# The first half's work up to FFN layer h1 ahead of the branch on exact weights, and FFN weights loaded in place

## The reference

```python
x = x + attn(xn) + ffn(xn)

def attn(h):                     # gated linear attention, keys 64, inner width 512
    x, final_gate = h @ up_w.T, h @ gate_w.T
    shift = silu(causal_conv4(x, conv_w) + conv_b)
    q, k = shift @ q_w.T, shift @ k_w.T
    v = sigmoid(x @ ig_w1.T @ ig_w2.T + ig_b2) * x
    g, tau = softplus(shift @ g_w.T + g_b), sigmoid(shift @ tau_w.T + tau_b)
    kn = k / norm(k) * g ** tau
    o = chunk_scan(q * 64 ** -0.5, kn, v, -g * tau) + shift * residual_weight
    xg = o * silu(final_gate)
    return (xg * rsqrt(mean(xg ** 2) + eps) * norm_weight) @ down_w.T

def ffn(h):                      # weights are -1, 0 or 1; s are scales per output
    h = silu(h @ w1.T * s1) * (h @ w2.T * s2)      # 256 -> 1024
    h = gelu(h @ h1.T * sh1)                       # 1024 -> 1024
    h = gelu(h @ h2.T * sh2)                       # 1024 -> 1024
    return h @ w3.T * s3                           # 1024 -> 256
```

## Time and profile before

| | |
|---|---|
| median of three runs | 1940.59 us |
| lowest, highest | 1940.5, 1941.85 us |
| profiled execution: its time, its span | 1940.21, 1938.4 us |
| TensorE busy | 1921.8 us (99%), 16804 matmuls |
| VectorE busy | 1584.1 us (82%) |
| ScalarE busy | 1295.3 us (67%) |
| granted TensorE clock, mean | 0.998 |

### The profile page before, as it was taken

How to read it: one execution, slowest core, us unless ns; L and a number is a source line. 1 busy time by engine, 2 the same in 40 slices (tenths; PEclk the granted TensorE clock), 3 DMA queues, 4 the chain that set the end, 5 groups by cost and what they waited for, 6 DMA issues and landing times.

```text
span 1938.4 us, 46120 instructions
## 1 busy us (share of the span) xinstructions
PE 1921.8 (99%) x16804; PEld 1902.9 (98%) x16804; DVE 1584.1 (82%) x4304; ACT 1295.3 (67%) x2687; POOL 81.2 (4%) x136
## 2 busy tenths in 40 slices
PE   8999999999999999999999999999999999999998
PEld 7999999999999999999999999999999999999998
DVE  7788888888788887888888788787888878888887
ACT  5666667767676766666766667675667666667575
POOL 0000000000000000000000000000000000000000
PEclk9999999999999999999999999999999999999999
DMA  8000000000000000000000000000000000000000
GB/s 309 7 12 13 12 2 12 12 12 12 13 1 12 13 12 12 8 5 13 12 13 12 7 6 12 13 12 13 1 12 13 12 12 12 1 13 12 13 7 8
DMA packets 23538, 34.19 MB, mean 18 GB/s; under 512 B 3170, under 2 KB 19810, under 8 KB 23364
## 3 DMA queue, kind: packets, MB, share of 16 engines
q1 hardware_dynamic: 23364, 31.43, 4.8%
HBM read 23.04 MB, written 8.39 MB: 16 GB/s over the span
## 4 chain that ended last, share of the span: by engine, by line
PE 94%; issue 2%; ACT 1%; DVE 1%; SPq 1%; DMA 0%; POOLq 0%; POOL 0%; DVEq 0%; ACTq 0%
PE fb L383 64%; PE ab L383 21%; PE ab L593 2%; PE ab L628 1%; PE ab L529 1%; PE ab L453 1%; PE ab L518 1%; PE ab L583 1%; PE fb L678 1%; SPq L289 0%; PE ab L590 0%; PE ab L469 0%; PE ab L606 0%; ACT wwhole L726 0%; DMA sgate<-stage_w 0%
## 5 line engine op out<-in xcount | busy, mean ns | idle before, releaser
L383 PE MATMUL fb<-hid1h,wwhole 128*128 128x256 f32 x2048 | 474.2, 279 | 0.1
L383 PE MATMUL fb<-hid1l,wwhole 128*128 128x256 f32 x2048 | 467.9, 276 | 0.0
L383 PE MATMUL fb<-hid0l,wwhole 128*128 128x256 f32 x2048 | 465.9, 276 | 0.0
L383 PE MATMUL fb<-hid0h,wwhole 128*128 128x256 f32 x2048 | 465.8, 276 | 0.0
L383 PEld LDWEIGHTS fb<-hid1h,wwhole 128*128 128x128 f32 x2048 | 384.5, 188 | 4.0 <-ACT raw L838 0.3
L383 PEld LDWEIGHTS fb<-hid1l,wwhole 128*128 128x128 f32 x2048 | 384.7, 188 | 0.0
L383 PEld LDWEIGHTS fb<-hid0h,wwhole 128*128 128x128 f32 x2048 | 384.5, 188 | 0.0
L383 PEld LDWEIGHTS fb<-hid0l,wwhole 128*128 128x128 f32 x2048 | 384.4, 188 | 0.0
L838 ACT ACTIVATE raw<-fb,sh_s 128x256 f32<-128x256 f32 x512 | 212.3, 465 | 150.3 <-PE fb L383 142.7
L383 PE MATMUL fb<-xntl,wwhole 128*128 128x256 f32 x1024 | 237.5, 276 | 0.0
L383 PE MATMUL fb<-xnth,wwhole 128*128 128x256 f32 x1024 | 237.5, 276 | 0.0
(11 more groups left out here) (234 smaller groups left out, 4481.6 us busy)
## 6 DMA issues: line engine op xcount, KB each, us to landing
xin<-x SPq DMA_DIRECT2D x32, 256.0 KB, 2.7
out<-xin SPq DMA_DIRECT2D x32, 256.0 KB, 2.2
stage_more<-stage_w SPq DMA_DIRECT2D x6, 512.0 KB, 7.1
sgate<-stage_w SPq DMA_DIRECT2D x4, 512.0 KB, 4.4
shift<-stage_w SPq DMA_DIRECT2D x4, 512.0 KB, 5.0
v<-stage_w SPq DMA_DIRECT2D x4, 512.0 KB, 5.6
raw<-stage_w SPq DMA_DIRECT2D x3, 512.0 KB, 6.0
mixed<-stage_w SPq DMA_DIRECT2D x3, 512.0 KB, 8.2
```

Source lines behind the costliest of these rows:

```text
L383: mm = pe.matmul(o, a, b, start=start and i == 0, stop=stop and i == len(pairs) - 1)
```

## The change

SP issues all chunks without a wait, each to a place of its own: the FFN chunks to where their rounded form will be (`wplain` is the plain f32 view of `wwhole`), the others to `stage` (over `hid1h`, `hid1l`) and `small`. Comb and gate move to the front of the order. Constants are split: 14 early ones two behind each of the first seven chunks, seven late ones one behind each later chunk.

A half is cut in two functions on each engine. `before` runs from z to proj, `after` from h1 to the end. For the first half `before` stands ahead of the branch, with some differences (`first`): layer1 multiplies the plain f32 weights by the plain f32 `xplain` (one plain matmul in place of two rounded ones), gate stands ahead of layer1, and ScalarE and VectorE have tests and roundings between its steps. The loops run `after`, `before` for each half. The unread matmuls are gone.

The test of an FFN chunk no longer compares with the rounded copy. It looks at the low 16 bits of each weight, read as uint16 with a step of two: ScalarE copies them to a scratch tile with their sum as accumulated output (`flag`, 18 chunks), or VectorE takes their maximum by a reduce (four chunks, `DVE_FLAGS`). A chunk whose low bits are all zero is exact. After its test a chunk is rounded in place by VectorE (`round_whole`). `ACT_FLAGS`, `ACT_LAST`, `DVE_ROUNDS` and `DVE_LAST` say which chunk is tested or rounded at which place. The late part, `ACT_LAST` and `DVE_LAST`, stands between `before` of the first half and the branch.

```diff
-CHUNKS = (["up"] + [f"w1{k}" for k in range(2)] + [f"w2{k}" for k in range(2)] + ["gate", "proj", "comb"]
+CHUNKS = (["up", "comb", "gate"] + [f"{w}{k}" for w in ("w1", "w2") for k in range(2)] + ["proj"]
           + [f"h1{k}" for k in range(8)] + ["down"] + [f"h2{k}" for k in range(8)] + ["w30", "w31"])
+ROUNDED = ("up", "comb", "gate", "proj", "down")
...
+ACT_FLAGS = {"first": ("w10", "w11", "w20", "w21"), 0: ("h10",), 1: ("h11",), 2: ("h12",), 3: ("h13",), 4: ("h14",), 5: ("h15",), 6: ("h16",)}
+ACT_LAST = ("h17", "down", "h20", "h22", "h23", "h25", "h26", "w30")
+DVE_ROUNDS = {1: ("h10",), 2: ("h11",), 3: ("h12",), 4: ("h13",), 5: ("h14",), 6: ("h15",), 7: ("h16",)}
+DVE_FLAGS = ("h21", "h24", "h27", "w31")
+DVE_LAST = ("tables", "w10", "w11", "w20", "w21", "h17", "down", "h21", "h20", "h22", "h24", "h23", "h27", "h25", "h26", "w31", "w30")
+ACT_FLAGGED = [name for names in (*ACT_FLAGS.values(), ACT_LAST) for name in names if name != "down"]
...
+        wplain = at_same_place("wplain", [P, len(WHOLE), STAGE], F32, wwhole_place)
...
-        stage_more = at_same_place("stage_more", [P, 2, STAGE], F32, hid1_place)
-        ig2raw = at_same_place("ig2raw", [ZK, DI], F32, hid1_place + 4 * FB * N)
+        stage = at_same_place("stage", [P, 4, STAGE], F32, hid1_place)
 
         mixed = sb("mixed", [P, 4 * N])
+        ig2raw = mixed[0:ZK, 0:DI]
...
+        xplain = work[:, DB * N:DB * N + HB * N].rearrange("p (h t) -> p h t", h=HB)
...
+        EARLY = ([(ident_s, ident), (ig1w, ig1t), (convw_s, convw), (convb_s, convb), (ig2raw[ZB:ZB + 1, :], ig2t[R:R + 1, :]),
+                  (ig2raw[ZB + 1:ZK, :], ig2t[R:R + 1, :])] + [(ig2raw[i * R:(i + 1) * R, :], ig2t[0:R, :]) for i in range(6)]
+                 + [(s1_s, s1), (s2_s, s2)])
+        LATE = [(projb_s, projb), (normw_s, normw), (resw_s, resw), (sh1_s, sh1), (sh2_s, sh2), (s3_s, s3),
+                (pair_mask, masks[:, LEVELS - 1, :])]
+
+        def stage_of(name):
+
+            if name == "comb":
+                return small[:, 0:STAGE]
+            return stage[:, ("up", "gate", "proj", "down").index(name), :] if name in SPLIT else wplain[:, WHOLE[name], :]
+
+        def low_bits(name):
+
+            return stage_of(name).bitcast(mybir.dt.uint16).rearrange("p (o two) -> p o two", two=2)[:, :, 0]
+
...
-            for n in range(len(CHUNKS)):
-                if n == SLOTS - 1:
-
+            early, late = iter(EARLY), iter(LATE)
+
+            def constants(some, count, landed):
+                for dst, src in itertools.islice(some, count):
+                    sp.dma_start(dst[:], src).then_inc(landed, 16)
+
+            for n, name in enumerate(CHUNKS):
+                sp.dma_start(stage_of(name), stage_w[n]).then_inc(stage_in[name], 16)
+                if name == "up":
                     sp.dma_start(xin[:, 0, :, :], x[0]).then_inc(x_in[0], 16)
-                    for dst, src in CONSTS:
-                        sp.dma_start(dst[:], src).then_inc(const_in, 16)
-                if n >= SLOTS:
-
-                    sp.wait_ge(prep_act, n - SLOTS + 1)
-                    sp.wait_ge(prep_dve, n - SLOTS + 1)
-                sp.dma_start(stage_slot(n), stage_w[n]).then_inc(stage_in[n % SLOTS], 16)
+                constants(early, 2, const_in)
+                if n >= len(EARLY) // 2:
+                    constants(late, 1, late_in)
...
-
-            def plain(bank, count, weights_at=0, moving_at=0):
-                for i in range(count):
-                    w, t = weights_at + (i // 2 % 6) * P, moving_at + (i % 2) * N
-                    pe.matmul(fb[bank][:, 0:N], up[:, w:w + P], w10[:, t:t + N], start=(i == 0), stop=(i == count - 1))
...
-                                   ig1w[:, d, :], start=(d == 0), stop=(d == DB - 1))
-            mm.then_inc(prep_pe, 1)
 
             def ln_transpose(me, first=False):
                 pe.wait_ge(xn_d.sem, xn_d.at(me))
@@ -453,16 +453,24 @@
                         mm = pe.transpose(ab[2][:, h * N + c * CH:h * N + (c + 1) * CH], xn[:, c, h * P:(h + 1) * P], ident_s[:])
                 mm.then_inc(ln_mm.sem, 1)
 
-            shifted(2, [(0, 48), (0, 64), (0, 80), (0, 96)])
+            pe.wait_ge(const_in, 16 * len(EARLY))
+            pe.wait_ge(stage_in["comb"], 16)
+            for h in range(HB):
+                for d in range(DB):
+                    mm = pe.matmul(ab[0][:, h * R:(h + 1) * R], stage_of("comb")[:, d * H + h * P:d * H + (h + 1) * P],
+                                   ig1w[:, d, :], start=(d == 0), stop=(d == DB - 1))
+            mm.then_inc(comb_mm, 1)
             ln_transpose((0, -1), True)
-            shifted(2, [(0, 112), (0, 128), (0, 8), (8, 8), (16, 0), (32, 0), (64, 0), (80, 160), (24, 104), (16, 96)])
-
-            def half(seq, p, last, exact):
+
+            def before(seq, p, exact, first=False):
                 me, prev = (seq, p), (seq, p - 1)
                 xh, xl = xnth, xntl
 
                 pe.wait_ge(ln_hi.sem, ln_hi.at(prev))
                 pe.wait_ge(ln_lo.sem, ln_lo.at(prev))
+                if first:
+                    pe.wait_ge(rounded_hi, is_rounded("comb"))
+                    pe.wait_ge(rounded_lo, is_rounded("comb"))
                 both = [combs[:, k, :, :].rearrange("p a r -> p (a r)") for k in range(HB)]
...
                             wb = ffn_weight(exact, w, k, m)
                             pairs += [(wb, a) for a in parts(exact, xh[:, k, :], xl[:, k, :])]
                         mm = wide(fb[m % 4][:, j * N:(j + 1) * N], pairs)
...
+                    gate(1)
+                    pe.wait_ge(xplain_d, 1)
+                    for k in range(HB):
+                        for w in ("w1", "w2"):
+                            pe.wait_ge(stage_in[f"{w}{k}"], 16)
                 for m in range(4):
                     layer1(m)
-                gate(0)
-                gate(1)
+                if not first:
+                    gate(0)
+                    gate(1)
 
                 def input_gate(c):
                     if c == 1:
...
             def sequences(exact):
                 with rounds(pe) as seq:
                     for p in range(HALVES):
-                        half(seq, p, False, exact)
-                for p in range(HALVES):
-                    half(B - 1, p, True, exact)
-
+                        after(seq, p, False, exact)
+                        before(seq, p + 1, exact)
+                after(B - 1, 0, True, exact)
+                before(B - 1, 1, exact)
+                after(B - 1, 1, True, exact)
+
+            before(0, 0, True, True)
...
+            def flag(name):
+
+                i = flagged[0] % 2
+                act.wait_ge(stage_in[name], 16)
+                if flagged[0] == 0:
+                    act.wait_ge(rounded_lo, is_rounded("gate"))
+                if flagged[0] > 1:
+                    act.wait_ge(flag_act, flagged[0] - 1)
+                act.activation(flag_out[:, i, :], low_bits(name), ACT.Copy,
+                               accum_out=inexact[:, WHOLE[name]:WHOLE[name] + 1]).then_inc(flag_act, 1)
+                flagged[0] += 1
...
+                if not first:
+                    act.preload_act_table_set("silu_and_others")
+                else:
+                    act.wait_ge(zs_one, 1)
...
                 def silu(m):
                     if m == 0:
                         act.wait_ge(fin_d.sem, fin_d.at(prev, 3))
+                    if m == 0 and first:
+                        act.wait_ge(ig2_d, 3)
...
+                if first:
+                    flags("first")
+                    round_high("proj")
                 for m in range(4):
                     silu(m)
+                    flags(m)
                 gate(0)
                 hid0(0)
                 act.wait_ge(conv_d.sem, conv_d.at(me))
                 act.activation(shift[:], shift[:], ACT.Silu).then_inc(shift_d.sem, 1)
                 silu(4)
+                flags(4)
                 act.wait_ge(shift_d.sem, shift_d.at(me))
...
+                flags(5)
                 silu(6)
+                flags(6)
                 silu(7)
...
+            def after(seq, p, last):
+                me = (seq, p)
...
-            act.wait_ge(prep_dve, len(CHUNKS))
+            act.preload_act_table_set("silu_and_others")
+            for name in ("up", "comb", "gate"):
+                round_high(name)
+            act.wait_ge(ln_mm.sem, ln_mm.at((0, -1)))
+            act.activation(xplain, ab[2][:].rearrange("p (h t) -> p h t", h=HB), ACT.Copy).then_inc(xplain_d, 1)
+            ln_high((0, -1))
+            before(0, 0, True)
+            for name in ACT_LAST:
+                if name == "down":
+                    round_high(name)
+                else:
+                    flag(name)
+            act.wait_ge(projb_d, 1)
...
+            def round_whole(name):
+
+                if name in DVE_FLAGS:
+                    dve.wait_ge(stage_in[name], 16)
```

(50 more changed lines are left out.)

185 lines of the change are left out of this document (83 added, 102 removed).

## The result

The changed kernel takes 1973.53 us (1972.65 to 1974.68, 4 runs) against 1940.55: ratio 1.0172, 95% interval 1.0158 to 1.0185. It is 33 us slower. The forecast was 3.4 us slower, with a range to 1951, so it was wrong by 30 us. All times are medians; two executions stand far outside and at a low clock, one of s4's six (2405 us) and one of the 15 of the kernel before that s1 to s4 are compared with (2760 us), and both count in the medians and are left out of the ratios.

A forecast was written before the change was run, and what follows sets the result against it. TensorE, busy 99%, bounds the kernel, so only the stretch ahead of h1 can change. h1 starting 1.45 us later plus 1.9 us of low clock gave 3.4 us slower, 1944.0 us from the median; range 1937 to 1951.

The forecast's parts named there:

- a turn costs nothing: Loops turning between proj and h1: read from ScalarE's square and table load 0.02 us apart at the old turn; no cost.
- Rival D: Loop's new turn costs over its 0.9 us of VectorE and ScalarE cover: 0.4 x 15 = 6 us more, 1950; chance 0.04.
- Constants: Start of the kernel: TensorE's wait for 14 early constants and comb ends at 13.8 us, bounds 13.0 and 14.9.
- Up's second half: First half, ahead of gate: up's first half ends at 23.7 us, its second at 25.3.
- The low clock behind the idle stretch: At h1, after TensorE idled over 20 us: four us at half speed lose 1.9 us, bounds 1.6 and 3.2.
- comb's 16 matmuls: TensorE's first work: nearly double the earlier 1.93 us, so 3.5 us, bounds 1.9 and 3.9.
- the stall ahead of gate: First half, behind up: TensorE idles 2.9 us for z's low part, so gate starts at 28.2 us.
- VectorE's tail: Ahead of the branch: 15 copies, 4 reduces, down's low part and tables, 17.2 us in sum, last copy ending at 69.9.
- Rivals B and C: VectorE's tail: B, reduce at 2.01 us, +6.6, 1947.2, chance 0.14; C, in-place copy at 1.15, 8.1 more, 1952, chance 0.06.
- the 3.4 us of the sum: Whole kernel: h1 1.45 us later plus 1.9 us of low clock, 3.4 us slower, 1944.0 us.
- if the period of a half is no longer 58.8: Steady rounds: sign that the forecast is wrong; 58.8 us a half was expected to stay.

The follow-up runs named there:

- s4: The changed kernel with TensorE's loop head set at slot 32 of its instruction fetch block: 1948.04 us, ratio 1.0037.
- s1: The kernel before, its turn in the old place, with TensorE's loop head set at slot 139 of its fetch block: 1978.23 us, ratio 1.0189.
- s7: s4 with the 14 early constants issued five behind each of the first three chunks, not two behind each of seven: 1942.60 us, ratio 1.0006.
- s6: The changed kernel with TensorE's loop head at slot 160, its branch at about the 24th instruction of its fetch block: 1986.71 us, ratio 1.0229.

## Why the prediction was wrong

- **"a turn costs nothing"** is the step that failed, in the paragraph "At no cost". It was read from ScalarE, whose branch indeed takes 0.05 us, and carried over to TensorE. What the runs show in its place is a branch of TensorE that takes 2.2 to 3.7 us and ends 2.3 to 2.7 us behind the start of an instruction fetch, longer than its queued matmuls last. The row of its own branch in the kernel before (915 ns, shown above) was there to be read: 0.9 us is nothing like ScalarE's, and a fetch that leads by 1.7 us is a cover that can be lost. The forecast had no term for it. It cost 24.5 us, and s4 gave 25.5 back.
- **Rival D** named the right place with the wrong mechanism. It looked for a chain over VectorE and ScalarE with 0.9 us to spare, priced 0.4 us a turn (times 15, where the loop turns 14 times), and got chance 0.04. Measured: 1.75 us a turn, by the fetch. The 0.9 us of that chain were never called on: in s4 all engines turn there at no cost.
- **Constants**: forecast 13.8 (bounds to 14.9), measured 17.2, outside the bounds. SP's issue was as reckoned; the last small constant landed 6.7 us after its issue at 10.5. The price from issue to landing had been taken from comb, 3.5 us. Seven chunks had been issued ahead of it; in s7, with three ahead, the last one lands 2.8 us after its issue at 8.4, so what it waits behind is read as the chunks. s7 also shows that the delay went through to the end.
- **Up's second half**: forecast 1.6 us, as if the clock had risen behind the first; all 24 matmuls ran at the 0.213 us pitch, so it took 2.6. With the constants' 3.4, gate's 0.5 and the tail's 0.5 less, this is how h1 comes 4.3 us later than the forecast's 71.8. In s4's execution the pitch fell to 0.113 within up, and its h1 starts 2.3 us sooner. The 1.2 GHz of the prediction is an estimate from this pitch (256 / 0.213 = 1.2 columns a ns); no view gives a clock in GHz. In the kernel before the pitch is 0.213 us at a granted clock of 0.50 (52.2 to 54.7 us) and 0.113 at 1.00 (168.8 to 170.0); in the changed kernel up has 0.213 at a granted clock of 1.00 (26 to 29 us).
- **The low clock behind the idle stretch**: 1.9 forecast, 2.4 measured, inside the bounds.
- **Right**: comb's 16 matmuls 3.5 (3.6 measured), the stall ahead of gate 2.9 (3.0), plain f32 layer1 0.213 us an instruction (6.92 / 32 = 0.216), ScalarE's test at 1.1 (pitch 1.04), the copy at 0.61 from start to start, reduces at 1.2 (1.209), VectorE's tail of 17.2 (16.7). Gate was 4.1 and took 4.6. ScalarE full and TensorE idle behind proj are as foretold, later by the terms above: idle from 55.4 to h1 at 76.1 (but for the branch's own two matmuls), where 49 to 72 was forecast.
- **Rivals B and C** are refuted: a test takes 1.2 us, and copies follow one another at 0.60 to 0.63 us in the chain of waits (B priced 2.01, C 1.15, the pitch of the two-input rows; no run shows the cycle that C speaks of):

```profile
L1026 DVE TENSOR_REDUCE inexact<-wplain x4: 1204/1209/1211, 62.8 to 71.4; 128x1 f32<-128x1024 uint16 x4
L1030 DVE CAST wwhole<-wplain x22: 677/682/694, 41.9 to 73.2; 128x1024 fp32r<-128x1024 f32 x22
```

- Without the turn the kernel is 7.6 us slower (s4), which the range to 1951 would have held. That is the width of the range; the 3.4 us of the sum were less than half of it.
- The text's own sign for being wrong, "if the period of a half is no longer 58.8", came: 59.6 on average. The other, h1 after 76, came by a hair, at 76.08.

## What to carry to other kernels

In a loop of some thousand instructions, look at the engine's own branch rows and at when the instruction fetch starts before costing a turn: 0.36 us and 3.6 us are the same instruction. Code that is added or removed ahead of such a loop moves the branch in its fetch block (by 13 slots here), and the slot alone was worth up to 39 us (s6 against s4); pin the loop's head (early in its block, with the branch well behind the start of its own) before comparing two versions, or the comparison measures the alignment. A row of one engine is no price for another.

## What the runs showed of the hardware

- A taken back branch of TensorE takes 0.34 to 0.49 us with the fetch 3 us or more ahead, 0.4 to 0.7 with it 2 to 3 us ahead, 0.7 to 1.5 with it 0.8 to 1.7 ahead, and 2.2 to 3.8 with it at or behind the branch. TensorE works off its queue meanwhile (branch at 193.86, last queued matmul at 195.66), so the changed kernel's gaps are 0.6 to 2.0 us.
- The cost of a gap is more than the gap: in the changed kernel the gaps sum to 15.5 us over 14 turns and the rounds are 24.5 longer. From the first start to the last, the first 128 matmuls of h1 take 14.4 us without a gap (s4); behind a gap they take 14.5 in seven turns, 15.0 in six, and 16.1 in one, where the granted clock is 0.50 for 3.4 us.
- The clock ahead of the branch differs between executions of the same code, and moves h1 by some 2 us (73.7 in s4's profile, 75.7 to 76.1 in four others).
- An early small transfer landed 6.7 us after its issue when seven 512 KB chunks were issued ahead of it, and 2.8 us after it with three ahead.
- GpSimd copies 128x1024 f32 to the rounded type in 1.04 us (median), 1.5 beside VectorE's copies, and VectorE is up to 2.2 times as slow beside it (1.53 against 0.69), by instruction.
